# One-hot row sets of the edge count: every second set built by GpSimd instead of VectorE

## The reference

```
src = concat([s, d, loop]); dst = concat([d, s, loop])
o = argsort(dst, stable=True); src = src[o]; dst = dst[o]
...
x = layernorm(x + gat0(x, src, dst))                 # 12 heads of 64
x = layernorm(x + gat_stack1(x, src, dst))           # 4 heads of 256, then one head of 768
```

## Time and profile before

| | |
|---|---|
| time, median of 3 runs | 1126.23 us (1125.57 to 1126.36) |
| the profiled execution's own time | 1124.05 us |
| its span, first to last instruction | 1122.3 us |
| first row set on VectorE to the last `add` | 10.57 to 79.04 us |
| VectorE busy over the span | 952.9 us (85%) |
| TensorE busy over the span | 1052.4 us (94%) |
| GpSimd busy over the span | 142.6 us (13%) |
| TensorE clock granted, mean | 0.992 of full speed |

### The profile page before, as it was taken

One profiled execution on the slowest core, in us unless ns is written; L12 is line 12 of the kernel. 1 busy time (PEld: TensorE's weight loads), 2 busy tenths in 40 slices (PEclk: granted clock), 3 DMA queues, 4 the chain that ended last, 5 costly groups with the idle time before them and its releaser, 6 DMA issues.

```text
span 1122.3 us, 20577 instructions
## 1 busy us (share of the span) xinstructions
PE 1052.4 (94%) x8048; PEld 905.6 (81%) x8048; DVE 952.9 (85%) x1531; ACT 642.5 (57%) x939; POOL 142.6 (13%) x155
## 2 busy tenths in 40 slices
PE   6986999898989899999999999999999999999996
PEld 4665666666666667999999999999988888888885
DVE  7989999999999999977853999999987874497865
ACT  8658999999999997223111567666612311234331
POOL 1000000000000000010073112020400153311111
PEclk9998999999999999999999999999999999999998
DMA  4061020202020205533237310204041124343211
GB/s 150 1 235 44 3 92 1 93 1 92 2 92 1 98 1 197 171 101 120 80 107 267 124 47 1 84 1 151 20 169 57 44 95 174 131 162 126 78 60 53
DMA packets 40022, 98.99 MB, mean 88 GB/s; under 512 B 4505, under 2 KB 17393, under 8 KB 39925
## 3 DMA queue, kind: packets, MB, share of 16 engines
q1 hardware_dynamic: 39926, 97.66, 24.9%
HBM read 70.74 MB, written 26.90 MB: 87 GB/s over the span
## 4 chain that ended last, share of the span: by engine, by line
PE 61%; DVE 20%; ACT 9%; issue 8%; DMA 1%; DVEq 1%; POOL 0%; SPq 0%; POOLq 0%; ACTq 0%
PE psum L1110 14%; PE psum L1019 13%; PE psum L1071 12%; DVE R L1692 9%; PE psum L1149 8%; DVE R L1678 5%; ACT R L1288 5%; PE psum L1034 4%; ACT R L1304 3%; PE psum L759 2%; PE psum L1087 1%; PE psum L944 1%; DVE LC L1664 1%; PE psum L1140 1%; PE psum L1122 1%
## 5 line engine op out<-in xcount | busy, mean ns | idle before, releaser
L944 PE MATMUL psum<-ident,R 128*128 128x128 f32 (+3 forms) x1200 | 156.8, 279 | 38.3 <-ACT R L1288 37.8
L944 PEld LDWEIGHTS psum<-ident,R 128*128 128x128 f32 (+3 forms) x1200 | 127.5, 142 | 78.9 <-ACT R L1288 66.5
L1692 DVE CUSTOM_DVE_ANT_0 R<-R,LC 128x1250 f32<-128x1250 f32 x120 | 175.1, 1462 | 0.2 <-DVE LC L1664 0.2
L1288 ACT ACTIVATE R<-R,row_max 128x1250 f32<-128x1250 f32 x120 | 161.6, 1347 | 2.0 <-DVE row_max L1692 1.6
L958 PE MATMUL psum<-R 128*64 128x256 f32 (+3 forms) x1200 | 147.2, 383 | 0.6 <-ACT R L1304 0.6
L1304 ACT COPY R<-psum 128x1280 f32<-128x1280 f32 x120 | 143.7, 1198 | 1.5 <-PE psum L944 1.5
L1019 PE MATMUL psum<-w_hi,x1T_hi 128*128 128x256 f32 (+1 forms) x480 | 128.6, 283 | 0.7 <-DVE x1T_lo L1784 0.7
L1019 PE MATMUL psum<-w_hi,x1T_lo 128*128 128x256 f32 (+1 forms) x480 | 127.3, 280 | 0.0
L1019 PE MATMUL psum<-w_lo,x1T_hi 128*128 128x256 f32 (+1 forms) x480 | 125.7, 281 | 0.0
L1678 DVE SCALAR_TENSOR_TENSOR R<-R 128x1250 f32<-128x1250 f32 x80 | 121.9, 1525 | 0.0
L2177 POOL TENSOR_TENSOR rstd<-rstd,minus_half 128x1 f32<-128x1 f32 (+1 forms) x40 | 33.9, 847 | 664.1 <-DVE rstd L1707 664.1
(11 more groups left out here) (234 smaller groups left out, 2482.9 us busy)
## 6 DMA issues: line engine op xcount, KB each, us to landing
R<-rows_spill SPq DMA_DIRECT2D x20, 625.0 KB, 5.2
rowbuf<-rows_spill SPq DMA_DIRECT2D x14, 625.0 KB, 5.2
lc_spill<-LC SPq DMA_DIRECT2D x9, 625.0 KB
LC<-lc_spill SPq DMA_DIRECT2D x9, 625.0 KB, 5.6
res_spill<-colbuf SPq DMA_DIRECT2D x36, 128.0 KB, 3.3
R<-res_spill SPq DMA_DIRECT2D x9, 512.0 KB, 3.5
R<-in_x_dram SPq DMA_DIRECT2D x1, 3456.0 KB
res_spill<-R SPq DMA_DIRECT2D x9, 384.0 KB
```

The costliest lines, as they stand in the source:

```text
L944: last = e.transpose(turn0[r % 2][0:m, s, 0:n_dst], ring[0:n_dst, r % RING0, s * P:s * P + m], ident[0:n_dst, 0:n_dst])
L1288: e.activation(ring[0:m, r % RING0, :], ring[0:m, r % RING0, :], ACT.Exp, bias=row_max[0:m, r % RING:r % RING + 1], scale=-1.0, accum_out= ...
L1692: e.tensor_tensor_reduce(slot, slot, LC[0:m, i, :], -1.0, MIN_CEILING, ALU.add, ALU.min, row_max[0:m, r % RING:r % RING + 1]).then_inc(S.l ...
```

## The change

Of the 17 row sets the eight with odd numbers are now made by GpSimd. It makes a set as ten comparisons of 128 columns, each against one value per partition, into a layout of its own (`[PAIR, P]`, a tile's 128 columns side by side, where VectorE's sets have them ten apart). Odd sets and even sets have one buffer each in place of two shared ones. For the comparison's value a float32 copy of `src_row` is made on VectorE. GpSimd starts set 1 when `prep` has reached `src_row`, and a later set `q` when TensorE has read all of set `q - 2`; TensorE waits on a new semaphore, `odd_rows`, ahead of the matmuls of an odd pair.

```diff
-        hot_rows = [edge_view([P, PAIR], BF16, EP) for _ in range(2)]
+        even_rows = edge_view([P, PAIR], BF16, EP)
+        odd_rows = edge_view([PAIR, P], BF16, EP)
...
+        src_row_f = edge_view([ET], F32, EP)
...
+        S.odd_rows = sem("odd_rows_ready")
...
+        PREP_ROW = 12
...
         def windows_pe(e, g, tiles):
             if g >= 2 and tiles[0] == 0:
                 e.wait_ge(S.win_added, g - 1)
+            if g // 2 % 2:
+                e.wait_ge(S.odd_rows, g // 4 + 1)
             for j in tiles:
                 e.wait_ge(S.win_hot, g * GT + j + 1)
-                hot_row = hot_rows[g // 2 % 2][:, :, g % 2 * GT + j]
+                hot_row = odd_rows[:, g % 2 * GT + j, :] if g // 2 % 2 else even_rows[:, :, g % 2 * GT + j]
...
             for g in range(GROUPS):
-                if g and g % 2 == 0:
+                if g and g % 4 == 0:
                     rows_of_pair(g // 2)
...
             def rows_of_pair(q):
-                e.tensor_tensor(hot_rows[q % 2], iota_rows, src_row[:, q * PAIR:(q + 1) * PAIR].unsqueeze(1).to_broadcast(
+                e.tensor_tensor(even_rows, iota_rows, src_row[:, q * PAIR:(q + 1) * PAIR].unsqueeze(1).to_broadcast(
                     [EP, P, PAIR]), ALU.is_equal)
...
+            e.tensor_copy(src_row_f, row_i)
             e.tensor_copy(src_row, row_i).then_inc(S.prep, 1)
...
+            e.wait_ge(S.cleared, 1)
+            e.wait_ge(S.prep, PREP_ROW)
+            for q in range(1, ET // PAIR, 2):
+                if q >= 2:
+                    e.wait_ge(S.win_free, PAIR * (q - 1))
+                for j in range(PAIR):
+                    last = e.tensor_scalar(odd_rows[:, j, :], iota_h[0:EP, 0:P],
+                                           src_row_f[:, q * PAIR + j:q * PAIR + j + 1], None, ALU.is_equal)
+                last.then_inc(S.odd_rows, 1)
```

More of the change, by code:

```diff
@@ L777, in all_pe @@
             e.wait_ge(S.win_kept, KEPT)
+            e.wait_ge(S.odd_rows, ET // PAIR // 2)
             for g in range(HT):
```

## The result

The changed kernel takes 1146.7 us (median of 4 runs, 1144.77 to 1148.16); the kernel before, on the same chip, 1125.9 (4 runs, 1123.93 to 1126.36). The ratio is 1.0186, with a 95% interval of 1.0174 to 1.0199: 20.8 us slower. The forecast was slower too, but by 5 us, and its range ended at 1140.

The account below looks back on a forecast made before the run. VectorE and TensorE bound the count together, both full in its first half. Seven rounds at +0.87 us gave 6.1, less 1.5 into idle time, rounded to +5: median 1131.3 us, range 1123 to 1140.

Parts of the forecast that it names:

- Eight row sets leave VectorE: Counting stage: 0.73 us each, 5.9 us in all; TensorE's pace leaves some 2.5 to 3 us, in the second half.
- A comparison on GpSimd: Odd sets in the count: 0.29 us from an `AFFINE_SELECT` row, 0.37 as other end from half a two-operand subtraction.
- The price of neighbourhood: VectorE's cells in the count: each GpSimd comparison holds the next cell 0.16 us; bounds nothing and 0.24.
- side sum for a hold of the whole 0.29 us: Count: if each comparison cost VectorE 0.29 us in place of 0.16, the sum would be about 13 us, not 5.
- It just fits, or is late by a tenth or two ... I count nothing here.: TensorE's wait for odd sets: GpSimd has 4.8 us from release to use and needs 4.1 to 4.9; counted as nothing.
- The rival of late sets: Count: GpSimd, held behind cells, has sets ready after 6.4 to 6.9 us; TensorE waits; +11, 1137.4 us; chance 0.18.
- GpSimd fits in: Count: comparisons don't hold cells, VectorE regains 0.73 us, TensorE sets the pace: -3 us, 1123.2; chance of faster 0.21.
- Even: Count: a hold of about 0.07 us, or idle time absorbing more, cancels the gain: 1126 to 1128 us; chance 0.19.
- The marks it named: Count: cells about 0.4 us apart, comparisons 0.3 alone, first-half row sets some 7.7 apart, last add at about 84.
- the late rival's two marks: Count: matmuls of odd pairs wait for GpSimd by more than 1 us each, and cells keep their 0.25 us.
- Layout, float32 copy: Weight load hidden behind a longer matmul, nothing counted; preparation's extra cast hidden under ScalarE's clearing, 0.17 us if uncovered.

Follow-up runs that it names:

- all sets still on VectorE: Kernel before, VectorE making all 17 sets, with GpSimd making the same eighty comparisons into a buffer no one reads: 1129.61 us against 1125.63, ratio 1.0037.
- the experiment with seven comparisons: Changed kernel with seven of ten comparisons in each odd set but the first: 1131.78 us against 1125.83 for the kernel before, ratio 1.0055.
- the kernel without odd sets: Against the kernel before: nobody makes the odd sets, odd pairs read the even ones' rows: 1125.88 us against 1126.89, ratio 0.9995.
- the kernel with the powers: Kernel before, with TensorE waiting ahead of every odd pair for twelve one-column powers on GpSimd; VectorE makes all sets: 1159.44 us against 1125.63, ratio 1.0299.

## Why the prediction was wrong

Its direction was right, its size too small by a factor of four, and the mechanism that it counted, VectorE and GpSimd holding each other, is only the smaller part of the loss. Step by step:

- *Eight row sets leave VectorE, ceiling 2.5 to 3 us.* The reading of TensorE's pace was right and the ceiling still too high: free of charge it is 1.0 us, with an interval that includes zero. The 5 us for which weight loads waited in the second half were the two engines' turns; with VectorE relieved, 4.0 of them were still there.
- *A comparison on GpSimd, 0.29 us, at most 0.37.* **This term was mis-sized first.** It is 0.60 alone and 0.64 in the count (the median; up to 1.27 where a row set of VectorE runs beside it). The nearest row by shape was of another instruction, and half of a two-operand row of 256 columns took its fixed part, about 0.2 us by the products of 128 and 1,280 columns (424 and 2318 ns), as if it halved with the columns. The range was closed on both sides by rows that did not bound it.
- *The price of neighbourhood, 0.16 us a comparison.* About 0.11 was measured, beside comparisons twice as long: inside the bounds. The round, forecast at 0.16 x 10 - 0.73 = 0.87 us more, comes to 0.4 by that price. The side sum for a hold of the whole 0.29 us was also off: by the prediction's own recipe it gives 11.6, not 13. The two kernels that keep VectorE supplied show what is left of the whole term: +1.1 us with the second buffer, +4 with all sets still on VectorE.
- *"It just fits, or is late by a tenth or two ... I count nothing here."* **This is the step that failed.** A set needed 6.0 to 7.2 us, not 4.9, by the price above. And the lead from release to use was read once, in the first half, as 4.8 us; in the second half, where the blocks stand shifted by a group, it is 3.6. The seven waits were 0.95 to 3.73 us, 13.6 in all, where the forecast had put nothing; its range, up to 1140, had room for the rival's 11 us and not for 20. Behind the wait stood everything that the prediction listed, and it was paid in full.
- *The rival of late sets* (+11 us, chance 0.18) has the right place: the same wait, the same seven rounds, and a point from which it decides, 4.8 us a set, that the experiment with seven comparisons found near that place. Its cause was wrong. GpSimd is not starved of turns by VectorE; beside cells, a comparison takes 0.64 us and alone 0.60. That it had a set ready after 6.4 to 6.9 us, close to the measured 6.0 to 7.2, is luck: it added 4 us of standing behind cells to ten comparisons at half their price. It counted 7 x 1.6 = 11.2 us of waits from the first half's lead, and 13.6 were seen; the rest of the 20 is what follows a wait, the half clock for one.
- *"GpSimd fits in", -3 us, and "Even".* Ruled out, the first by the kernel without odd sets: even there nothing comes out ahead.
- *The marks it named.* Cells at 0.4 us apart beside GpSimd: 0.31. Comparisons at 0.3 alone: 0.60. Row sets 7.7 us apart in the first half: they are 7.1 and 8.8. The last add at about 84: 98.80. Of the late rival's two marks the profile has one, odd matmuls that wait over 1 us (six of the seven); the other, cells that keep 0.25 us, it hasn't (0.31).
- *Layout, float32 copy.* Nothing of either is seen: VectorE makes the first add at 16.12, against 16.11 before, and the kernel with a second buffer, which has both, loses 1.1 us in all.
- *The clock* was in no step. Waits of 3.73 and 2.62 us were followed by 1.2 GHz, in the rounds of 14.4 and 12.3 us. With the clock held at 2.4 GHz the loss was 18.8 us (1145.72 - 1126.89) in place of 20.8; its exact share is open, and differs from execution to execution.

The sum as the runs give it: the neighbour and VectorE's relief together +1.1 us (second buffer); the series, with the clock that falls because of it, 20.8 - 1.1 = 19.7 us, of which the clock is some 2 to 4 us (an estimate, from the medians and from the count with every wait filled).

## What to carry to other kernels

Before work goes to another engine behind a single buffer, write the round as two times in a row, maker plus reader, and compare it with the round that was; the price of the maker has to come from the same instruction on the same engine, and where no row has it, the range is open at that end. Read the lead from release to use at every place where the interleaving shifts, not once. Two buffers, or a handover in halves of the same one, made 19 to 20 of 21 us vanish; but look first whether the relief buys anything, since an engine that is full beside another that is full gives nothing back.

## What the runs showed of the hardware

- A comparison on GpSimd (float16 to bfloat16, against one value per partition) costs 0.29 us and 2.5 ns a column, with the engine alone; a product of 128 columns takes 0.42 us, of 1,280 columns 2.32 us, so the two-operand product is faster by the column than the one-operand comparison.
- One product of 1,280 columns on GpSimd held a 480-column cell of VectorE for nearly its own whole length (2.2 of 2.59 us), but ten comparisons of 128 columns, 0.64 us each, slow the cells only by 0.055 us each, and powers of one column, 0.6 us each, not at all (five cells in 1.35 us). The Trainium skill (SBUF — State Buffer, Who interferes with whom) has an exclusive lock for the whole instruction; the long product agrees with it. The short comparisons don't: with it, each would hold a cell for most of its 0.6 us, and they cost about 0.11. Why isn't known from these runs.
- TensorE was granted 1.2 GHz during a stand-still of 3.73 us, and again after one of 2.62; the other five, of 0.95 to 1.81 us, in the same execution left it at 2.4 GHz. The same wait filled with matmuls on zeros kept it there. The length of one stand-still doesn't decide it by itself: of two of 3.07 us one after the other (the kernel with the powers), the first left the clock at 2.4 GHz and the second did not, and beside the long product it fell at 35.2 us, after a stand-still of 1.68.
- At the start of the count the first record of 2.4 GHz came at 15.7 to 21.2 us, in kernels that hardly differ up to there, and window matmuls before it took 0.44 us each, later 0.22. Two profiled executions can differ by 2 us for this alone.
